# A graph and expert network on one core: rows sent as 112 and 13, and expert results scattered by token instead of stored by place and fetched by place

## The chip, the cores and the metric

The kernel runs on one core of one Trainium2 chip. The metric is the device time of one launch in microseconds (us). Before the change it is 2292.94 us, the median of three runs (2292.32 to 2293.6).

## The reference

Four blocks act on 1250 tokens of 512 features, each added to the running `x` after a layer norm. The change touches what carries rows in and out, and the second block, whose routing is this:

```python
x = x + gnn0(layernorm(x), edge_index, ...)        # graph sum, two layers with batch norm
x = x + ffn0(layernorm(x)[None], gate_w, experts)  # the block below
x = x + gnn1(layernorm(x), edge_weight, weight, src, dst)
x = x + ffn1(layernorm(x)[None], ...)              # tree of 8 leaves, 512 -> 2048 -> 512 each

# ffn0: N = 1250 tokens, 8 experts, m = N // 8 = 156 places each
cg = sinkhorn(gates)                                # 8 rounds
vals, idx = top_k(cg.T, m)                          # each expert picks 156 tokens
gate_values = vals > 0.5
outputs = einsum(routed_tokens[idx], experts) * gate_values
s = zeros(N, 512).at[idx].add(outputs)
c = zeros(N).at[idx].add(1.0)
out = s / (c + 1)
```

A plan value above 0.5 can hold for one expert only, so a token has at most one expert whose result counts. Every other row of the sum has the weight 0.

## The kernel before

A token tile is 125 rows (`TR`), and there are ten of them (`NT`). The kernel is a chain of phases, each an `nc.Block()`: in it every engine has its own program, written out by hand, and all engines meet at a barrier at its end. The order of the work is the order in which each engine's program is written. DMAs that are issued by SyncE (`sp`) run through one queue, q1, in the order of the code; those of ScalarE through q10; GpSimd's indirect ones (`q.indirect_dma_start`), whose rows are chosen by indices in SBUF, through q0.

**`phase_edges`** (L180). SyncE issues loads of constants and edges, then five loads of `x`, two tiles each (L243, `x_rows`). VectorE meanwhile builds the one-hot rows of the edges up to L308. **`phase_adjacency`** (L348) first needs all of `x`: VectorE waits for `x_loaded` and then reads its loop bounds into registers (L376), TensorE reads its bounds first and then waits for `x_loaded` (L425). TensorE then does eight small matmuls (L426), four transposes (L430), and multiplies the one-hot rows that VectorE makes (L394, L399) at L446 and L453.

**`phase_route`** (L950) makes the normalised rows `c_rows` and stores them, ten stores of one tile (L1287), into the DRAM tensor `c_d`. Its VectorE chain makes the plan, the 1280 places (8 experts of 160) and, at the end, `token_of`: which token sits at each place (L1154 to L1156), and `place_from`: at which place each token's result will lie (L1136). Empty places hold the token number 0.

**`phase_experts`** (L1374). GpSimd gathers the rows of the 1280 places from `c_d` with ten indirect DMAs of 128 rows (L1411). TensorE turns a group (`turn_x`, L1525), and works through 16 chunks of 80 places, two for each expert. Chunk `c` is evicted by ScalarE into slot `c % 4` of `y_rows` (L1458), which from chunk 4 on waits for the slot's last DMA. SyncE stores each chunk plainly to `results_d` by place (L1434). When all 16 have landed, GpSimd fetches with ten indirect DMAs of 125 rows the result of each token by its place (L1418), VectorE adds it, times the token's `share`, to `x_rows` (L1506), and the norm and the second graph sum follow (`Gather1`): its first TensorE work waits for the first tile's `A_lo` (L1333). The share is 0 for a token without an expert.

**`phase_tree`** (L1625) is the long rest. Its last step adds into `x_rows` tile by tile (L2287), and `store_out` (L1744) stores each tile as it is done, eight from SyncE's queue and two from ScalarE's.

## Time and profile before

| what | value |
|---|---|
| median of three runs | 2292.94 us (2292.32 to 2293.6) |
| the profiled execution | 2290.14 us |
| its span, first to last instruction | 2288.2 us |
| TensorE busy | 2168.5 us, 95% |
| VectorE busy | 1587.5 us, 69% |
| GpSimd busy | 623.0 us, 27% |
| TensorE's granted clock, mean | 0.979 of full |

A span is read from the first to the last instruction of one profiled execution; what lies outside it (here 1.9 us) belongs to the launch. TensorE is busy nearly all the time from 600 us on, where the tree begins. The stages that the change touches are short: the first 31 us, the stretch from 440 to 525 us, and the last 5 us.

### The profile page before, as it was taken

The numbers are of one execution on the slowest core, as the hardware profiler recorded it, in microseconds if no ns is written. First come the engines' busy times: TensorE is split into PE (matmuls) and PEld (weight loads), VectorE is DVE, ScalarE is ACT, GpSimd is POOL, SyncE is SP. The second block draws the span as 40 slices with busy tenths as digits, with TensorE's granted clock in tenths as the row PEclk, the third lists the DMA queues.
The fourth block names the chain that finished last, engine by engine and source line by source line (L and its number), as shares of the span: only waits on it lengthen the run. The fifth ranks groups of instructions, "written<-read, shape, count | busy, mean of one in ns | idle before, by whom it ended". The sixth has DMA issues, their size and how long they took to land.

```text
span 2288.2 us, 32770 instructions
## 1 busy us (share of the span) xinstructions
PE 2168.5 (95%) x11859; PEld 1901.6 (83%) x11859; DVE 1587.5 (69%) x2606; ACT 1068.2 (47%) x1857; POOL 623.0 (27%) x1066
## 2 busy tenths in 40 slices
PE   5897998588999999999999999999999999999999
PEld 4887996458858888888888888888888888888887
DVE  7994356636477667777776677777766777777665
ACT  4335335345364444455544444555444445554443
POOL 1553000111112322233223222332233223323320
PEclk9999998598999999999999999999999999999999
DMA  2000202251001111111111111111111111111111
GB/s 72 3 2 1 74 1 80 72 162 37 28 24 55 38 42 37 56 38 42 39 54 42 37 38 56 42 38 41 57 38 37 38 61 37 37 45 54 38 37 55
DMA packets 70720, 101.99 MB, mean 45 GB/s; under 512 B 5539, under 2 KB 40947, under 8 KB 70563
## 3 DMA queue, kind: packets, MB, share of 16 engines
q1 hardware_dynamic: 67263, 94.20, 12.7%
q0 software_dynamic: 3040, 5.19, 0.8%
q8 instruction: 97, 1.59, 0.3%
q10 hardware_dynamic: 260, 0.51, 0.1%
q14 instruction: 60, 0.49, 0.1%
HBM read 92.14 MB, written 7.74 MB: 44 GB/s over the span
## 4 chain that ended last, share of the span: by engine, by line
PE 73%; DVE 0%; ACT 0%; DMA 0%; issue 0%
PE psum L548 24%; PE psum L549 24%; PE psum L550 24%; PE psum L2140 1%; PE psum L2033 0%; PE psum L2023 0%; DMA w_raw<-in_w 0%; DVE w_lo L2195 0%; ACT w_forms_hi L1875 0%; PE psum L2040 0%; ACT w_hi L1884 0%; DVE x_rows L2287 0%; ACT f_rows L542 0%; DVE x_rows L2319 0%; DVE stats L506 0%
## 5 line engine op out<-in xcount | busy, mean ns | idle before, releaser
L548 PE MATMUL psum<-w_hi,hidden_hi 128*125 128x512 f32 x1280 | 503.4, 393 | 2.6 <-issue 2.4
L550 PE MATMUL psum<-w_hi,hidden_lo 128*125 128x512 f32 x1280 | 504.5, 394 | 0.0
L549 PE MATMUL psum<-w_lo,hidden_hi 128*125 128x512 f32 x1280 | 504.3, 394 | 0.0
L549 PE MATMUL psum<-x_forms_lo,w_forms_hi 128*128 128x418 f32 x1260 | 445.4, 354 | 0.0
L1816 POOL TENSOR_TENSOR w_forms<-w_raw 128x128 f32<-128x128 f32 x189 | 104.9, 584 | 1127.5 <-PE psum L550 580.2
L2287 DVE SCALAR_TENSOR_TENSOR x_rows<-psum,leaf_by_token,x_rows 125x512 f32<-125x512 f32 x320 | 233.9, 748 | 254.2 <-PE psum L550 254.2
L1913 ACT ACTIVATE hidden<-psum 128x418 f32<-128x418 f32 x315 | 162.0, 514 | 487.1 <-PE psum L550 484.9
L548 PEld LDWEIGHTS psum<-w_hi,hidden_hi 128*125 128x125 f32 x1280 | 237.4, 185 | 59.5 <-issue 3.0
L550 PEld LDWEIGHTS psum<-w_hi,hidden_lo 128*125 128x125 f32 x1280 | 236.7, 185 | 59.0
L549 PEld LDWEIGHTS psum<-w_lo,hidden_hi 128*125 128x125 f32 x1280 | 237.1, 185 | 54.1
L2260 DVE TENSOR_TENSOR hidden_lo<-hidden,hidden_hi 128x418 fp32r<-128x418 f32 (+1 forms) x384 | 255.0, 690 | 21.4 <-ACT hidden_hi L1935 21.4
L1925 ACT ACTIVATE hidden<-hidden,b1cols 128x414 f32<-128x414 f32 x315 | 201.4, 639 | 101.9 <-DVE hidden L2215 92.0
L549 PEld LDWEIGHTS psum<-x_forms_lo,w_forms_hi 128*128 128x128 f32 x1260 | 237.9, 189 | 7.7
L548 PE MATMUL psum<-x_forms_hi_late,w_forms_hi 128*128 128x418 f32 x630 | 224.1, 356 | 0.0
L548 PE MATMUL psum<-x_forms_hi_first,w_forms_hi 128*128 128x418 f32 x630 | 223.3, 355 | 0.7 <-DVE hidden L2204 0.7
L550 PE MATMUL psum<-x_forms_hi_first,w_forms_lo 128*128 128x418 f32 x630 | 222.1, 353 | 0.0
L1816 POOL TENSOR_TENSOR w_forms<-w_raw,w_forms 128x128 f32<-128x128 f32 x378 | 220.4, 590 | 4.9
L550 PE MATMUL psum<-x_forms_hi_late,w_forms_lo 128*128 128x418 f32 x630 | 221.6, 352 | 0.0
L1935 ACT ACTIVATE hidden_hi<-hidden 128x418 fp32r<-128x418 f32 (+1 forms) x384 | 204.2, 550 | 6.0
L2190 DVE TENSOR_TENSOR w_forms_lo<-w_forms,w_forms_hi 128x1792 fp32r<-128x1792 f32 x63 | 127.6, 2026 | 37.0 <-ACT w_forms_hi L1875 37.0
L1816 POOL TENSOR_TENSOR w_forms<-w_forms,w_raw 128x128 f32<-128x128 f32 x252 | 136.1, 540 | 4.9
L548 PEld LDWEIGHTS psum<-x_forms_hi_first,w_forms_hi 128*128 128x128 f32 x630 | 118.7, 188 | 8.7 <-DVE hidden L2204 1.0
(354 smaller groups left out, 3528.7 us busy)
## 6 DMA issues: line engine op xcount, KB each, us to landing
w_raw<-in_w SPq DMA_DIRECT2D x127, 512.0 KB, 3.8
expert_raw<-in_experts SPq DMA_DIRECT2D x8, 1024.0 KB, 5.5
expert_results_d<-expert_results SPq DMA_DIRECT2D x16, 160.0 KB, 4.4
x_rows<-in_x SPq DMA_DIRECT2D x5, 500.0 KB
c_rows_d<-c_rows SPq DMA_DIRECT2D x10, 250.0 KB
W_raw<-in_gnn_W SPq DMA_DIRECT2D x4, 512.0 KB, 4.1
W_raw<-in_gnn_W SPq DMA_DIRECT2D x1, 2048.0 KB, 9.7
b_by_token<-in_b SPq DMA_DIRECT2D x8, 256.0 KB, 3.8
```

The source lines that it names most:

```text
L548: t.matmul(out, stat[0], mov[0], start=start, stop=False, skip_group_check=again)
L549: t.matmul(out, stat[0], mov[1], start=False, stop=False, skip_group_check=again)
L550: return t.matmul(out, stat[1], mov[0], start=False, stop=stop, skip_group_check=again)
L1816: q.tensor_tensor(u[:, to, :], a, b, op).then_inc(w_sum, 1)
L1913: a.activation(slot_of(hid, G, b, j), g.psum[:, bank, 0:width(b)], ACT.Copy, scale=scale).then_inc(copied, 1)
L1925: a.activation(to, to, ACT.Gelu, bias=bias(G, j)).then_inc(active, 1)
L1935: a.activation(slot_of(hhi, G, b, j), slot_of(hid, G, b, j), ACT.Copy).then_inc(hi_cut, 1)
L2140: ins = t.matmul(g.psum[:, PLAIN_BANK[b][j], 0:hi - lo], g.wplain[:, k, j * 128:(j + 1) * 128], g.xf[:, k, lo:hi], start=k == 0, stop=k == ...
L2190: v.tensor_tensor(to[:, U1:U15 + 1, :], g.wsum[n % 2][:, U1:U15 + 1, :], of[:, U1:U15 + 1, :].bitcast(F32), ALU.subtract).then_inc(w_lo, 1)
L2260: v.tensor_tensor(slot_of(hlo, G, b, j), slot_of(hid, G, b, j), slot_of(hhi, G, b, j).bitcast(F32), ALU.subtract).then_inc(lo_cut, 1)
L2287: v.scalar_tensor_tensor(out=g.x_rows[:, i, :], in0=g.psum[0:TR, i % Y_BANKS, :], scalar=g.leaf[:, i, e:e + 1], in1=g.x_rows[:, i, :], op0 ...
```

## The change

Three things are changed.

1. Rows of a tile are sent as rows 0 to 111 and rows 112 to 124, in separate DMAs. The load of `x` is five DMAs of 112 rows by two tiles, and one of 13 rows by all ten. Each output tile is stored by two DMAs. The token rows that come back in the experts' phase are loaded in the same way.
2. `c_d` grows from 1250 rows to 2560. Rows 1250 to 2559 are filled from `c_rows` by two more stores in `phase_route` (values that nobody uses, but that are there), and GpSimd's first gather waits for them too.
3. A second table, `owner_of`, says for each place where its result goes: the token's own row of `c_d`, or, for an empty place, row 1280 + place. It takes four VectorE instructions at the end of `phase_route`; `place_from` goes. SyncE stores the table to DRAM and loads it back by chunk (80 by 16). After its gathers have landed, GpSimd scatters each evicted chunk into `c_d`, in place of SyncE's plain store, and SyncE then loads the ten tiles plainly from rows 0 to 1249. A token without an expert gets its normalised row back, and its share of 0 drops it.

```diff
+EVEN_ROWS = 112
+NOBODY = NG * 128
...
+            x_tiles = g.x.rearrange("(t p) d -> p t d", p=TR)
             for i in range(0, NT, 2):
-                sp.dma_start(g.x_rows[:, i:i + 2, :],
-                             g.x[i * TR:(i + 2) * TR, :].rearrange("(t p) d -> p t d", p=TR)).then_inc(g.x_loaded, 16)
+                sp.dma_start(g.x_rows[0:EVEN_ROWS, i:i + 2, :], x_tiles[0:EVEN_ROWS, i:i + 2, :]).then_inc(g.x_loaded, 16)
+            sp.dma_start(g.x_rows[EVEN_ROWS:TR, :, :], x_tiles[EVEN_ROWS:TR, :, :]).then_inc(g.x_loaded, 16)
...
-            s.mark(v.tensor_scalar(g.place_from[:, :], place[:, :], -1.0, 0.0, ALU.add, ALU.max))
...
-            s.mark(v.tensor_copy(g.token_of[:, :], token[:, :]))
+            s.mark(v.tensor_scalar(g.token_of[:, :], token[:, :], float(NOBODY), float(N - 1), ALU.add, ALU.min))
+            s.mark(v.tensor_scalar(spare[:, :], tables[:, C_G - C_Q:C_TOKEN - C_Q], 128.0, g.rowno[:, :], ALU.mult, ALU.add))
+            s.then(v.tensor_scalar(vacant[:, :], token[:, :], 0.0, None, ALU.is_equal))
+            s.then(v.tensor_tensor(spare[:, :], spare[:, :], vacant[:, :], ALU.mult))
+            s.mark(v.scalar_tensor_tensor(out=g.owner_of[:, :], in0=token[:, :], scalar=float(NOBODY), in1=spare[:, :],
+                                          op0=ALU.add, op1=ALU.add))
...
+            sp.dma_start(g.c_d[N:2 * N, :].rearrange("(t p) d -> p t d", p=TR), g.c_rows[:, :, :]).then_inc(g.c_stored, 16)
+            sp.dma_start(g.c_d[2 * N:NOBODY + NP, :], g.c_rows[0:NOBODY + NP - 2 * N, 0, :]).then_inc(g.c_stored, 16)
...
-            for i in range(4):
-                q.wait_ge(stored[i], 16 * 4)
-            q.wait_ge(x_lo, NG)
-            for t in range(NT):
-                q.indirect_dma_start(g.fetched_rows[:, t, :], None, g.results_d[:, :],
-                                     bass.IndirectOffsetOnAxis(ap=g.place_from[:, t:t + 1], axis=0),
-                                     bounds_check=NP - 1, oob_is_err=False).then_inc(fetched[t // 2], 16)
+            for i in range(NG // 2 + 1):
+                q.wait_ge(back[i], 16 if i < 2 else 32)
+            q.wait_ge(owners_in, 16)
+            for c in range(2 * NE):
+                q.wait_ge(copied, c + 1)
+                q.indirect_dma_start(g.c_d[:, :], bass.IndirectOffsetOnAxis(ap=g.owner_by_chunk[:, c:c + 1], axis=0),
+                                     g.y_rows[:, c % 4, :], None,
+                                     bounds_check=NOBODY + NP - 1, oob_is_err=False).then_inc(stored[c % 4], 16)
...
+            sp.dma_start(g.owner_d.rearrange("(g p) a -> p (g a)", p=128), g.owner_of[:, :],
+                         allow_slow_non_contiguous=True).then_inc(owners_out, 16)
+            sp.wait_ge(owners_out, 16)
+            sp.dma_start(g.owner_by_chunk[:, :], g.owner_d.rearrange("(c p) a -> p (c a)", p=CH),
+                         allow_slow_non_contiguous=True).then_inc(owners_in, 16)
...
-                sp.wait_ge(copied, c + 1)
-                sp.dma_start(g.results_d[c * CH:(c + 1) * CH, :], g.y_rows[:, c % 4, :]).then_inc(stored[c % 4], 16)
+            for i in range(4):
+                sp.wait_ge(stored[i], 16 * 4)
+            token_rows = g.c_d[0:N, :].rearrange("(t p) d -> p t d", p=TR)
+            for t in range(0, NT, 2):
+                for lo, hi in ((0, EVEN_ROWS), (EVEN_ROWS, TR)):
+                    sp.dma_start(g.fetched_rows[lo:hi, t:t + 2, :],
+                                 token_rows[lo:hi, t:t + 2, :]).then_inc(fetched[t // 2], 16)
...
     def store_out(eng, i):
         eng.wait_ge(y_added, y_count(LASTQ, i))
-        eng.dma_start(g.out[i * TR:(i + 1) * TR, :], g.x_rows[:, i, :]).then_inc(out_stored, 16)
+        for lo, hi in ((0, EVEN_ROWS), (EVEN_ROWS, TR)):
+            eng.dma_start(g.out[i * TR + lo:i * TR + hi, :], g.x_rows[lo:hi, i, :]).then_inc(out_stored, 16)
```

The order of SyncE's queue from `phase_route` to the end of the experts, before (line numbers are those of the kernel before) and then changed (its own line numbers):

```order
L1284 DMA place_tables<-in_consts_d 128x158
L1287 DMA c_rows_d<-c_rows 125x512 [waits c_normed] x10
L1290 DMA expert_raw<-in_experts 128x4x512 [waits r_w_lo] x2
L1434 DMA expert_results_d<-expert_results 80x512 [waits x_copied] x2
L1428 DMA expert_raw<-in_experts 128x4x512 [waits x_wlo]
L1432 DMA W_rows<-in_gnn_weight 128x4x512 [waits x_lo]
L1434 DMA expert_results_d<-expert_results 80x512 [waits x_copied] x6
```

```order
L1293 DMA place_tables<-in_consts_d 128x158
L1296 DMA c_rows_d<-c_rows 125x512 [waits c_normed] x10
L1297 DMA c_rows_d<-c_rows 125x10x512
L1298 DMA c_rows_d<-c_rows 60x512
L1301 DMA expert_raw<-in_experts 128x4x512 [waits r_w_lo] x2
L1438 DMA owner_of_place_d<-owner_of_place 128x10x1
L1441 DMA owner_by_chunk<-owner_of_place_d 80x16x1 [waits x_owners_out]
L1447 DMA expert_raw<-in_experts 128x4x512 [waits x_wlo] x4
L1451 DMA W_rows<-in_gnn_weight 128x4x512 [waits x_lo]
L1457 DMA fetched_rows<-c_rows_d 112x2x512 [waits x_stored2,x_stored3,x_stored1,x_stored0]
L1457 DMA fetched_rows<-c_rows_d 13x2x512
```

The chunk stores have left this queue (in the first piece the pair of chunks and one expert load stand once for four such turns), and two stores, the round trip of the owners and the plain loads have come in.

GpSimd's indirect DMAs in the experts' phase, before and then changed:

```order
L1407 UNCONDITIONAL_BRANCH [waits barrier_Pool_Activation_PE_DVE_SP_gather]
L1411 DMA rows_by_place<-c_rows_d,token_of_place 128x512 [waits c_stored]
L1411 DMA rows_by_place<-c_rows_d,token_of_place 128x512 x9
L1418 DMA fetched_rows<-expert_results_d,place_from 125x512 [waits x_stored3,x_stored2,x_lo,x_stored1,x_stored0]
L1418 DMA fetched_rows<-expert_results_d,place_from 125x512 x9
```

```order
L1420 UNCONDITIONAL_BRANCH [waits barrier_Pool_Activation_PE_DVE_SP_gather]
L1424 DMA rows_by_place<-c_rows_d,token_of_place 128x512 [waits c_stored]
L1424 DMA rows_by_place<-c_rows_d,token_of_place 128x512 x9
L1432 DMA c_rows_d<-expert_results,owner_by_chunk 2560x512 [waits x_back4,x_back5,x_back3,x_owners_in,x_back2,x_copied,x_back1,x_back0]
L1432 DMA c_rows_d<-expert_results,owner_by_chunk 2560x512 [waits x_copied] x15
```

The ten fetches have gone, and 16 scatters stand there, each behind the eviction of its own chunk; the first also waits for all gathers and for the owners.

The end of VectorE's program in `phase_route`, before and then changed:

```order
L1136 TENSOR_SCALAR place_from<-place 125x10
L1137 TENSOR_SCALAR place_i<-place 125x10
...
L1151 SCALAR_TENSOR_TENSOR share<-place,is_out 125x10
L1154 TENSOR_REDUCE token_of_place_f_8815<-psum 128x10
L1156 CAST token_of_place<-token_of_place_f_8815 128x10
```

```order
L1158 TENSOR_REDUCE token_of_place_f_8817<-psum 128x10
L1160 TENSOR_SCALAR token_of_place<-token_of_place_f_8817 128x10
L1161 TENSOR_SCALAR spare_row<-place_tables,small_consts 128x10
L1162 TENSOR_SCALAR vacant<-token_of_place_f_8817 128x10
L1163 TENSOR_TENSOR spare_row<-spare_row,vacant 128x10
L1164 SCALAR_TENSOR_TENSOR owner_of_place<-token_of_place_f_8817,spare_row 128x10
```

Behind the reduction L1154 stood one instruction, and now five do; the first row of the first piece is the one that goes.

## Rows read from the trace of the kernel before

**Rows 1.** The page: the span, and the chain that ended last by engine.

```profile
span 2288.2 us, 32770 instructions
PE 73%; DVE 0%; ACT 0%; DMA 0%; issue 0%
```

**Rows 2.** Waits (who, for whom: us, times, longest), 0 to 60, then 440 to 640.

```profile
PE psum L426 <- DMA x_rows<-in_x: 16.3, 1, 16.3
...
PE psum L548 <- DVE A_lo L1333: 17.5, 3, 16.9
```

**Rows 3.** Timeline 28 to 36 us: start, us, engine, line, operation.

```profile
28.39 0.27 DVE L308 COPY b1cols<-psum 128x128 f32<-128x128 f32 x1
30.86 1.85 PE L426 MATMUL psum<-gate,small_consts 128*125 128x8 f32 x8 [16.25 <-DMA x_rows<-in_x]
32.07 1.94 DVE L394 TENSOR_SCALAR src_onehot<-i,key 125x1280 bf16<-125x1280 f16 x4 [3.41 <-issue]
33.43 3.30 PE L446 MATMUL psum<-dst_onehot,src_onehot 125*128 x29
35.91 1.11 DVE L394 TENSOR_SCALAR src_onehot<-i,key 125x1280 bf16<-125x1280 f16 x2 [1.44 <-PE psum L446]
```

**Rows 4.** Line 376, the loads of loop bounds: ns min/median/max, first and last start.

```profile
L376 PEldq TENSOR_LOAD <-bounds x10: 587/592/781, 29.6 to 167.5; - x10
L376 DVEq TENSOR_LOAD <-bounds x10: 593/598/847, 30.8 to 165.8; - x10
```

**Rows 5.** Windows: busy PE, PEld, DVE, ACT, POOL; then PEclk, DMA share, GB/s.

```profile
8.00:10.00 2.00, 2.00 (x13) 1.71 (x12) 1.63 (x8) 0.46 (x1) 0.00 (x0) 1.00 0.46 56
28.00:30.00 2.00, 0.00 (x0) 0.00 (x0) 0.66 (x4) 0.00 (x0) 0.00 (x0) 1.00 0.33 128
506.60:507.40 0.80, 0.43 (x4) 0.19 (x2) 0.80 (x2) 0.80 (x3) 0.00 (x0) 1.00 0.70 202
```

**Rows 6.** DMA view of 8 to 10 us: packets by size.

```profile
DMA packets 690, 0.11 MB, mean 56 GB/s; under 512 B 558, under 2 KB 672, under 8 KB 690
```

**Rows 7.** The ten stores of `c_rows`: ns, first and last start.

```profile
L1287 SPq DMA_DIRECT2D c_rows_d<-c_rows x10: 250/251/505, 380.2 to 392.4; - x10
```

**Rows 8.** Timeline 441 to 461 us.

```profile
441.99 0.17 DVE L1136 TENSOR_SCALAR place_from<-place 125x10 int32<-125x10 f32 x1
442.07 0.17 DVE L1137 TENSOR_SCALAR place_i<-place 125x10 int32<-125x10 f32 x1
442.27 0.17 DVE L1138 TENSOR_SCALAR place_digits_i<-place_i 125x10 int32<-125x10 int32 x1
...
445.59 0.17 DVE L1156 CAST token_of_place<-token_of_place_f 128x10 int32<-128x10 f32 x1
446.89 1.20 POOL L1411 DMA_INDIRECT rows_by_place<-c_rows_d,token_of_place  x1 [68.88 <-issue]
450.57 1.12 PE L1525 MATMUL psum<-small_consts,rows_by_place 128*128 128x128 f32 x4 [5.23 <-DMA rows_by_place<-c_rows_d,token_of_place]
460.03 0.69 PE L1525 MATMUL psum<-small_consts,rows_by_place 128*128 128x128 f32 x4
```

**Rows 9.** Timeline from 473 us, one row of each queue or engine.

```profile
473.14 0.60 ACT L1458 ACTIVATE expert_results<-psum 80x512 f32<-80x512 f32 x1 [0.35 <-PE psum L550]
505.94 0.30 SPq L1434 DMA_DIRECT2D expert_results_d<-expert_results  x1
508.94 1.26 POOL L1418 DMA_INDIRECT fetched_rows<-expert_results_d,place_from  x1 [49.10 <-issue]
516.04 0.75 DVE L1506 SCALAR_TENSOR_TENSOR x_rows<-fetched_rows,share,x_rows 125x512 f32<-125x512 f32 x1 [7.13 <-DMA fetched_rows<-expert_results_d,place_from]
...
2283.89 0.26 SPq L1746 DMA_DIRECT2D out_rows<-x_rows  x1
```

**Rows 10.** The page's DMA issues: count, KB each, median us from issue to landing.

```profile
w_plain<-in_w SPq DMA_DIRECT2D x1, 512.0 KB, 3.4
rows_by_place<-c_rows_d,token_of_place POOLq DMA_INDIRECT x10, 3.8
```

**Rows 11.** Line 1434, the 16 chunk stores.

```profile
DMA to landing us min/median/max: 1.9/4.4/6.2
```

**Rows 12.** DMA view, 40 slices of 2280 to 2288.2 us.

```profile
GB/s 120 120 80 130 110 100 120 100 40 110 80 110 90 110 80 50 120 80 130 100 140 70 110 110 100 90 120 80 70 80 100 100 130 130 110 50 10 0 0 0
```

21 lines of the change are left out of this document (13 added, 8 removed).

## The prediction

> **What bounds the kernel now.** I read the chain of waits first, then the waits of the stretches that the change touches, then their timelines and windows. By the chain [rows 1] the kernel is TensorE's: 73% of the span are its matmuls, and nothing else has a whole per cent. The change leaves every matmul as it is. So it can only move the moments at which TensorE may start, and the moment at which the last store has landed. There are three such places. At the start TensorE waits 16.3 us for `x`; between the experts and the second graph sum it waits 16.9 us for the chain fetch, add, norm, `A_lo` [rows 2]; and the kernel ends with a store. A fourth, the gap between routing and the first gathered rows, is 5.2 us long [rows 8] and can only grow.
>
> **The start: 0.2 us gained.** The five loads of `x` run at 128 GB/s with a DMA share of 0.33 [rows 5], which is about 5 engines of 16. The 80-row store of 506.6 to 507.4 us has a share of 0.70 and 202 GB/s in a window that it doesn't fill. 125 is 5 times 25, 80 is 16 times 5: I infer from these rows that rows are shared out evenly over the largest number of engines up to 16 that divides them. Then 112 rows go over 16, 13 over 13, and the load takes about half its time: 2.56 MB in 10 to 12 us in place of 20, so that `x` is in SBUF by about 22 us in place of 30.8.
> The Trainium skill, "DMA: Bandwidth & Descriptors", section "Why a DMA increments its semaphore by 16 and not by 1", gives the same division rule. By it the 13 rows use 13 engines; the sum goes by the rows, which show only 125 and 80, and the case in which 13 behaves otherwise is a rival below.
> What is late then? VectorE ends the edges' phase at 28.66 us (28.39 + 0.27) [rows 3]. TensorE's load of loop bounds, which doesn't wait for `x`, starts at 29.6 us [rows 4]: it already shows how early the next phase can begin. With 0.6 us for the load and 0.4 for what follows (VectorE's load starts at 30.8, and its first instruction at 32.07, so 1.27 us in all, of which 0.6 is the load), TensorE is ready at about 30.65. It starts at 30.86 now. So 0.2 us is gained of 16.3. VectorE gains more: its load can start at 29.6 too, 1.2 us earlier. But VectorE has at once to wait for TensorE's first 20 matmuls (1.44 us, until 35.91) [rows 3], so that TensorE's start decides. I take 0.2; the ends are 0 and 1.2, VectorE's gain.
>
> **The end of routing: 0.5 us lost.** Chained small VectorE instructions follow each other by 0.20 us (442.07 to 442.27), unchained ones by 0.08 (441.99 to 442.07) [rows 8]. Behind `token_of` come four new ones, up to the end of `owner_of`: two at 0.08, two at 0.22 (the reduction at 445.37 and the copy at 445.59 stand 0.22 apart): 0.6 us. `place_from` gives back 0.08. All engines meet at the barrier behind it, so 0.5 us is on the path; ends 0.4 and 0.8.
>
> **The larger `c_d`: nothing.** 1310 more rows, 2.68 MB, over 5 engines at 128 GB/s: 20 to 21 us behind the ten stores, whose last is issued at 392.4 [rows 7] and has landed by about 404. They end near 425 and the gather starts at 446.89 [rows 8]: 20 us of slack is the cover. The load of the third expert, which stands behind them in the queue, isn't used before the experts' phase. Without that cover each us would be paid in full.
>
> **The round trip of the owners: 0.3 us lost.** 1280 packets of 4 bytes out and 1280 back, 80 for each of 16 engines. No such store stands in the trace. The nearest row is 8 to 10 us: 690 packets, 558 of them under 512 B, with a DMA share of 0.46, so 0.46 x 2 us x 16 / 690 = 21 ns for each [rows 5, 6]. The other end is a whole 2 KB packet: 2048 B at a fifth of 128 GB/s, 80 ns. Each DMA then takes 80 x 21 to 80 x 80 ns, 1.7 to 6.4 us, and about 1.5 us around it (the 80-row store, 5 packets for each engine, lands in 1.9 at best [rows 11]). The owners are in at 447 + 6.4 = 453 to 447 + 16 = 463 us. Nobody waits until the first scatter must have landed for chunk 4 to be evicted, at 473.14 [rows 9]. What is paid is the quarrel with the first gathers: TensorE waits for group 0 until 450.57 [rows 8], and its 8 packets for each engine share the engines with the store's. Some 8 small packets between them are 0.2 to 0.6 us: I take 0.3, ends 0 and 2. Later groups have slack, since group 2 is turned at 460.03 only [rows 8].
>
> **Scatter and plain load: 1.8 us gained.** Now: last store issued at 505.94, landed 1.9 us later, GpSimd's first fetch at 508.94, 1.1 us after the landing (behind the barrier too it needs 1.1: 446.89 against the end of VectorE's last instruction at 445.76 [rows 8]), VectorE at 516.04 [rows 9, 11]. Changed: GpSimd sees the last eviction at 505.9, just before the store's issue, and starts its scatter at 506.8 (I take 0.9, since one wait stands there in place of five). It lands as a gather does, after 3.8 us [rows 10]: 510.6. SyncE issues 112 x 2 and 13 x 2 rows, 512 KB together. `w_plain`, of the same size, lands in 3.4 us [rows 10]; 0.3 us for the second issue: 514.3. So 1.8 us earlier than 516.04. Ends: a scatter of 2.7 us (0.8 us of issue, and 1.9) and a load of 3.0 give 512.5, 3.5 us gained; a scatter as slow as the slowest chunk store, 6.2 us [rows 11], and a load of 4.5 give 517.5, 1.5 us lost. GpSimd's earlier scatters keep pace (about 2 us each against a chunk every 3.2 us). The later pairs come faster than VectorE takes them, and all behind it up to the tree moves as one piece.
>
> **The last store: 1.5 us gained.** 250 KB over 5 engines at about 100 GB/s are 2.5 us; the data ends at 2280 + 37 x 0.205 = 2287.6 [rows 12], and the span at 2288.2. Over 16 engines the 224 KB take 0.9 us at 250 GB/s, and the 13 rows one packet more behind an issue of 0.3 us. 2.5 - 0.9 gives 1.6, less what the second issue shows: 1.5. Ends 0.3 and 1.8.
>
> **The sum.** -0.2 + 0.5 + 0.3 - 1.8 - 1.5 = -2.7 us. The profiled execution takes 2290.14 us, so 2287.4 as profiled. The median of the runs stands 2.8 us above it, and the forecast goes with the median: 2292.94 - 2.7 = 2290.2. A measurement of this kernel tells 0.2%, 4.6 us, from no change; 2.7 us lies inside.
>
> **Rivals.**
> *Faster: the DMAs in the middle are short ones.* The fetch by index goes, and with 5 packets for each engine the scatter is nearer to the store's 1.9 us than to the gather's 3.8. For it speaks that a gather carries 128 rows and 0.2 us more of issue; against it, that the chunk stores' median is 4.4 us [rows 11]. Then 3.5 from the middle, 1.8 at the end and VectorE's 1.2 at the start, less 0.5: -6.0, 2286.9 us.
> *The 13 rows stay on one engine.* Then a pair's second DMA puts 26 packets behind 14: 40 x 80 ns = 3.2 us in place of 1.2, and the middle loses 0.2 in place of gaining 1.8. At the end 20 packets at 100 ns are 2.0 us, and 0.3 is left. The start has room (70 + 130 packets x 80 ns = 16 us from 10.3 is 26.3, before 29.6). Sum: -0.2 + 0.8 + 0.2 - 0.3 = +0.5, 2293.4 us. Against it: 125 rows don't stay on one engine either.
> *Slower: the owners come late and the ring of four fills.* The scatter of chunk 0 must be issued by 473.14 - 3.8 - 0.9 = 468.4. From 446.6, less 2 x 1.5 us, that leaves 18.8 us for 160 packets: at over 117 ns for each, ScalarE waits, and TensorE behind it. At 200 ns the owners come 13 us late, and the time is 2290.2 + 13 = 2303 us. The rows give 21 to 80 ns, but for no 4-byte store.
> The Trainium skill, "DMA: Bandwidth & Descriptors", section "Specifications", says that below 512 B a DMA engine does a read and a modified write. No row here shows what that costs; if it doubled the 80 ns of a whole packet to 160, the sum would be 7 us worse by it. This rule speaks against the change, and it is that rival's reason.
>
> **How the numbers follow.** My forecast has 0.61, the faster rival 0.22, one engine for 13 rows 0.09, late owners 0.08. The forecast's own range is 2287.6 to 2292.5. To leave no more than 2 in 10 out, the range goes down to the faster rival and up past the one-engine case: 2286.6 to 2294.0. Faster by over 0.2% (below 2288.4) is the faster rival and a strip of the forecast, 0.25; slower by over 0.2% (above 2297.5) is late owners, 0.08; the rest, 0.67, is within.
>
> **What would show it right or wrong.** Start: `x` landed by 22 us, first matmul at L426 (new line 429) near 30.65. Routing: the first gather 0.5 us after its old distance from the reduction. Owners: `owner_by_chunk` landed by 463. Middle: from the last eviction to VectorE's first add 8.4 us in place of 10.1. End: from the last add to the end 2.9 us in place of 4.4. The forecast is wrong if VectorE decides the start, if a scatter takes over 5 us, or if ScalarE waits for a scatter.

## The result, and the profile after

The changed kernel takes 2295.64 us (median of 20 runs, 2294.69 to 2298.22), the kernel before 2291.80 on the same chip (20 runs, 2290.58 to 2293.6): a ratio of 1.0019, interval 1.0013 to 1.0025. It is slower by 3.8 us. That is outside the range of the prediction, whose upper end was 2294.0, and the time moved the other way: forecast were 2.7 us less, from the median of three runs of the kernel before (2292.94), which lies 1.1 us above the median of twenty. The profiled executions are 2290.14 us before and 2295.32 us after, the spans 2288.2 and 2293.5. So the two profiles lie 5.2 us apart, the medians 3.8: the profiled execution of the kernel before is one of its faster ones, 1.7 us below its median, that of the kernel after is 0.3 below its own.

The page of the kernel after, span and chain, answers to [rows 1]: the chain is TensorE's as before.

```profile
span 2293.5 us, 32798 instructions
PE 73%; issue 0%; ACT 0%; DVE 0%
```

The timeline at the start answers to [rows 3], line 429 to the old 426:

```profile
28.11 0.27 DVE L311 COPY b1cols<-psum 128x128 f32<-128x128 f32 x1
30.01 1.94 DVE L397 TENSOR_SCALAR src_onehot<-i,key 125x1280 bf16<-125x1280 f16 x4 [1.63 <-issue]
30.37 1.84 PE L429 MATMUL psum<-gate,small_consts 128*125 128x8 f32 x8 [16.05 <-issue]
32.93 4.12 PE L449 MATMUL psum<-dst_onehot,src_onehot 125*128 x40
35.41 1.11 DVE L397 TENSOR_SCALAR src_onehot<-i,key 125x1280 bf16<-125x1280 f16 x2 [3.00 <-PE psum L449]
```

TensorE starts 0.5 us earlier, and what ends its wait is no longer the DMA of `x`. VectorE starts 2.06 us earlier and gives all but 0.5 of it back in the wait for TensorE (3.00 in place of 1.44).

The timeline from the end of routing to the first scatter answers to [rows 8] (1438 and 1441 are the store and the load of the owners, 1424 the gather, 1549 the first transposes, 1482 the eviction of a chunk, 1432 the scatter):

```profile
445.06 0.17 DVE L1160 TENSOR_SCALAR token_of_place<-token_of_place_f 128x10 int32<-128x10 f32 x1
446.12 0.37 SPq L1438 DMA_DIRECT2D owner_of_place_d<-owner_of_place  x1
446.97 1.21 POOL L1424 DMA_INDIRECT rows_by_place<-c_rows_d,token_of_place  x1 [69.31 <-issue]
456.55 0.34 SPq L1441 DMA_DIRECT2D owner_by_chunk<-owner_of_place_d  x1
459.44 2.05 PE L1549 MATMUL psum<-small_consts,rows_by_place 128*128 128x128 f32 x8 [14.62 <-DMA rows_by_place<-c_rows_d,token_of_place]
467.63 0.59 ACT L1482 ACTIVATE expert_results<-psum 80x512 f32<-80x512 f32 x1 [5.51 <-PE psum L553]
470.78 0.93 POOL L1432 DMA_INDIRECT c_rows_d<-expert_results,owner_by_chunk  x1 [10.85 <-DMA owner_by_chunk<-owner_of_place_d]
480.45 0.60 ACT L1482 ACTIVATE expert_results<-psum 80x512 f32<-80x512 f32 x1 [0.35 <-PE psum L553]
```

Here is the loss. The gather is issued at 446.97, where it was before (446.89), but TensorE gets its first rows at 459.44 in place of 450.57: 8.9 us late. The fifth eviction stands at 480.45 against 473.14 [rows 9], 7.3 us later, and from there on everything is. (The 1.6 us between the two figures are the granted clock: at its half level until 7.2 us behind the first transposes here, 459.44 to 466.6, and until 9.6 us behind them before, 450.57 to 460.2.) What ends the wait of the fifth eviction is TensorE ("<-PE psum"), and by the view of the scatters (line 1432) no eviction waited for one. From issue to landing, the views of lines 1424, 1438 and 1441 give, in this order (minimum, median, maximum):

```profile
DMA to landing us min/median/max: 10.4/11.2/12.4
DMA to landing us min/median/max: 10.4/10.4/10.4
DMA to landing us min/median/max: 13.2/13.2/13.2
```

A gather took 3.8 us in the median before [rows 10]. The DMA view of the same 12 us, 446 to 458, says what the engines were busy with (queue: packets, MB, share of the time of 16 engines; `q0` carries the gathers, `q1` the DMAs of SyncE). Before:

```profile
DMA packets 554, 1.83 MB, mean 152 GB/s; under 512 B 108, under 2 KB 108, under 8 KB 554
q0 software_dynamic: 554, 1.83, 51.0%
```

After:

```profile
q0 software_dynamic: 86, 0.32, 69.7%
q1 hardware_dynamic: 1296, 0.01, 4.9%
```

A packet of the gathers' queue takes 0.51 x 192 / 554 = 0.18 us in the mean before (12 us of 16 engines are 192 us) and 0.697 x 192 / 86 = 1.56 us after. The packets of the 4-byte store themselves are charged with 0.049 x 192 / 1296 = 0.007 us. The small store is cheap by its own packets; what it costs stands in the packets of the others.

The mean hides how. The gathers' large packets carry 4096 B each, and the trace has the time of every one. Of those that start in these 12 us, the 446 before take 0.16 us in the median and 0.85 at most; the 78 after take 0.83 in the median, and six of them 6.6 to 8.3 us. The store's own packets all start between 447.02 and 447.84, and yet it lands only at 456.5. So a few packets stand still for as long as the store takes to land.

The middle, timeline, answers to [rows 9]:

```profile
512.62 0.59 ACT L1482 ACTIVATE expert_results<-psum 80x512 f32<-80x512 f32 x1 [2.18 <-PE psum L553]
514.01 0.91 POOL L1432 DMA_INDIRECT c_rows_d<-expert_results,owner_by_chunk  x1 [1.86 <-ACT expert_results L1482]
516.70 4.52 SPq L1457 DMA_DIRECT2D fetched_rows<-c_rows_d  x10
520.84 0.75 DVE L1530 SCALAR_TENSOR_TENSOR x_rows<-fetched_rows,share,x_rows 125x512 f32<-125x512 f32 x1 [4.62 <-DMA fetched_rows<-c_rows_d]
528.43 0.69 PE L551 MATMUL psum<-A_hi,d_rows_hi 125*128 125x418 f32 x1 [14.10 <-DVE A_lo L1344]
```

From the start of the last eviction to VectorE's first add it is 520.84 - 512.62 = 8.22 us; before it was 516.04 - 505.31 = 10.73. The wait of TensorE for `A_lo` falls from 16.9 us [rows 2] to 14.1. The scatter and the plain load do what was forecast, and more: 2.5 us.

The end, the last add of the tree (VectorE, line 2312):

```profile
2290.07 0.75 DVE L2312 SCALAR_TENSOR_TENSOR x_rows<-psum,leaf_by_token,x_rows 125x512 f32<-125x512 f32 x1 [2.04 <-PE psum L553]
```

From its start to the end of the span it is 3.43 us; before, from 2283.11 to 2288.2, it was 5.09. So 1.66 us gained.

One piece is left. From TensorE's first matmul of the middle to the last add, where nothing was changed, it takes 2283.11 - 523.92 = 1759.19 us before and 2290.07 - 528.43 = 1761.64 after: 2.45 us more. The timeline of TensorE shows it just behind a pause in the last steps of the second graph sum, where the tree begins. Before:

```profile
636.02 0.62 PE L2023 MATMUL psum<-small_consts,f_rows 125*128 125x125 f32 x4 [2.23 <-issue]
636.47 2.98 PE L2140 MATMUL psum<-f_xT,w_plain 128*128 128x418 f32 x8
```

After:

```profile
640.32 0.72 PE L2048 MATMUL psum<-small_consts,f_rows 125*128 125x125 f32 x4 [2.23 <-issue]
640.83 4.61 PE L2165 MATMUL psum<-f_xT,w_plain 128*128 128x418 f32 x8
```

The same eight matmuls after the same pause take 4.61 us in place of 2.98. The windows of the kernel after (columns as in [rows 5]: busy PE, PEld, DVE, ACT, POOL, then the granted clock of TensorE) show the clock at its half level, 1.2 of 2.4 GHz, in two stretches behind pauses:

```profile
638.10:640.30 2.20, 0.00 (x0) 0.02 (x1) 1.62 (x8) 1.14 (x3) 0.00 (x0) 1.00 0.00 0
640.70:644.10 3.40, 3.40 (x8) 1.82 (x6) 3.31 (x8) 2.05 (x4) 0.00 (x0) 0.50 0.00 0
...
685.07:688.48 3.41, 3.22 (x8) 2.56 (x9) 2.60 (x6) 0.00 (x0) 0.00 (x0) 0.50 0.49 153
```

The second stands behind a pause of 2.35 us. The kernel before has both pauses (2.23 and 2.36 us) and no such stretch behind either. Its window:

```profile
637.70:641.10 3.40, 3.40 (x13) 1.92 (x13) 2.20 (x5) 1.35 (x3) 0.00 (x0) 1.00 0.00 0
```

Both kernels have one more stretch at half clock between the middle and the last add, 3.41 us long, from 600.16 before and from 603.15 after; it cancels in the comparison.

In the profiled executions the sum is: +7.3 up to the last eviction, -2.5 to the first add, -0.3 to the first matmul, +2.45 to the last add, -1.7 to the end: +5.3 us.

### The profile page after: what moved, and what is told of

The parts are those of the page before. It is cut to its first block, busy times and chain, and to the rows that moved or that the text cites. A ratio compares the mean times of both kernels' runs of the same rounds, so it can differ in the third digit from the quotient of the medians.

```text
span 2293.5 us, 32798 instructions
## 1 busy us (share of the span) xinstructions
PE 2170.1 (95%) x11859; PEld 1902.5 (83%) x11859; DVE 1587.7 (69%) x2609; ACT 1068.3 (47%) x1857; POOL 627.9 (27%) x1072
## 4 chain that ended last, share of the span: by engine, by line
PE 73%; issue 0%; ACT 0%; DVE 0%
PE psum L551 24%; PE psum L552 24%; PE psum L553 24%; PE psum L2165 1%; PE psum L2058 0%; PE psum L2048 0%; ACT w_forms_hi L1900 0%; PE psum L2065 0%; DVE x_rows L2312 0%; ACT f_rows L545 0%; DVE x_rows L2344 0%; DVE stats L509 0%; DVE hidden L2229 0%; ACT w_forms_hi L1898 0%; ACT w_forms_hi L1896 0%
```

## Experiments

Times are medians, with the number of runs; each ratio is to the kernel before in the runs of the same chip (2291.57, 2291.81 and 2291.60 us in the three groups e1 to e4, e5 to e8 and e9 to e12). The theory at the start: the round trip of the owner numbers in packets of 4 bytes holds up the gathers, and all the rest of the change gains.

### e1: the kernel before with the rows split, and nothing else

```diff
...
+                sp.dma_start(g.x_rows[0:EVEN_ROWS, i:i + 2, :], x_tiles[0:EVEN_ROWS, i:i + 2, :]).then_inc(g.x_loaded, 16)
+            sp.dma_start(g.x_rows[EVEN_ROWS:TR, :, :], x_tiles[EVEN_ROWS:TR, :, :]).then_inc(g.x_loaded, 16)
...
+        for lo, hi in ((0, EVEN_ROWS), (EVEN_ROWS, TR)):
+            eng.dma_start(g.out[i * TR + lo:i * TR + hi, :], g.x_rows[lo:hi, i, :]).then_inc(out_stored, 16)
```

> The kernel before with the 112 and 13 rows at the load of x and at the output stores only. Theory (the split gains at both ends, as the trace after shows it: first edge matmuls 0.5 us earlier, 3.4 in place of 5.1 us from the last add to the end): 2.2 us less than before, ratio 0.9990, gathers land in 3.8 us. Rival (the two ends gain nothing by themselves, and the changed kernel's shorter end comes from something else): no difference, tail 5.1 us. Second rival (the doubled number of output DMAs disturbs the tree's weight loads): slower than before.

2288.61 us (11 runs, 2287.04 to 2290.40), ratio 0.9987 (0.9978 to 0.9996): 3.0 us faster. The profile has the first matmuls of the edges at 33.00 (33.43 before [rows 3]) and 3.4 us from the last add to the end (5.09): 2.1 of the 3.0 us. The split is a gain by itself.

### e2, e5: the kernel before with the store of the owners' size, and half of it

Nobody reads what it stores and nobody waits for it before the last chunk.

```diff
         def _(sp):
+            sp.dma_start(g.owner_d.rearrange("(g p) a -> p (g a)", p=128)[:, 0:10], g.token_of[:, 0:10],
+                         allow_slow_non_contiguous=True).then_inc(owners_out, 16)
```

> The kernel before with nothing but the store of 1280 four-byte numbers added at the start of the experts' phase (token_of goes out; nobody reads it and nobody waits for it until the phase's end). Theory (these packets hold the DMA engines against the gathers): the store lands after about 10 us, the first gather lands at 8 to 11 us in place of 3.6, TensorE's first transpose waits 12 to 15 us in place of 5.2, and the time is 7 us above before. Rival (the larger c_d, whose rows are gathered, or its 2.7 MB of extra stores, make the gathers slow): gathers land in 3.8 us and the time is that of before, within 1 us.

2297.94 us (6 runs, 2296.28 to 2298.54), ratio 1.0029 (1.0017 to 1.0041): 6.4 us slower. The store lands after 11.2 us, the gathers after 5.4, 8.1 and 10.6. TensorE, in the timeline of e2:

```profile
447.44 0.37 SPq L1425 DMA_DIRECT2D owner_of_place_d<-token_of_place  x1
458.85 1.11 PE L1529 MATMUL psum<-small_consts,rows_by_place 128*128 128x128 f32 x4 [12.10 <-DMA rows_by_place<-c_rows_d,token_of_place]
```

One instruction that nobody waits for brings the whole loss. Is it the number of packets? In e5 the slices are `[:, 0:5]`: 640 packets in place of 1280.

> The kernel before with half of the store added: five of the ten columns, 640 four-byte packets. Theory (the cost goes by the number of small packets): the store lands after about 6 us in place of 11.2, the first gathers are late by half as much, time 3 to 4 us above before. Rival (any strided store of this kind blocks the engines for a fixed time): 6 to 7 us above before, as with 1280.

2298.39 us (6 runs, 2297.55 to 2301.14), ratio 1.0034 (1.0021 to 1.0046). Half the packets, the same loss: the store lands after 11.5 us, the gathers after up to 11.5. The timeline of e5:

```profile
446.39 0.37 SPq L1425 DMA_DIRECT2D owner_of_place_d<-token_of_place  x1
458.82 1.97 PE L1529 MATMUL psum<-small_consts,rows_by_place 128*128 128x128 f32 x8 [13.12 <-DMA rows_by_place<-c_rows_d,token_of_place]
```

Between 640 and 1280 packets the cost doesn't go with their number, and so the way in which the prediction priced the store (a time for each packet, times 80) is wrong. In both runs, too, most of the gathers' 4096 B packets of 446 to 458 us are as fast as before (0.16 to 0.18 us in the median), and single ones take up to 7.5 us (e2) and 7.2 us (e5).

### e6: the kernel before with a load of 1280 numbers of 4 bytes

```diff
...
+            sp.dma_start(g.dummy[:, :], g.b1.rearrange("e h -> (e h)")[0:NP].rearrange("(g p) -> p g", p=128),
+                         allow_slow_non_contiguous=True).then_inc(owners_out, 16)
```

> The kernel before with a load of 1280 four-byte numbers from DRAM at the start of the experts' phase, which nobody uses, in place of the store. Theory (a small packet costs its time whichever way it goes): lands after 6 to 10 us, gathers late, time 3 to 7 us above before. Rival (only small writes to DRAM are slow, since less than a full burst is read and written back): the load lands in 3 to 4 us, gathers in 3.8 to 4.5 us, time within 1 us of before.

2291.55 us (10 runs, 2290.22 to 2293.75), ratio 1.0001 (0.9991 to 1.0010). The DMA view, 446 to 458 us, of e6:

```profile
q0 software_dynamic: 526, 1.75, 51.6%
q1 hardware_dynamic: 1296, 0.01, 5.0%
```

1296 packets again, with nearly the same share as in the kernel after, at the same moment; but the gathers' packets stay at 0.516 x 192 / 526 = 0.19 us. The load lands in 2.2 us and the first transposes start at 450.96. So it isn't small packets as such: it is small packets that are written to DRAM. The Trainium skill, "DMA: Bandwidth & Descriptors", section "Specifications", says that below 512 B a DMA engine reads and writes back. The costly store of e2 fits that; the row makes no difference between a store and a load, though, and the load of e6 pays nothing. The page gives no price, and that the price falls on the other queue's packets isn't in that section. The same page, section "Back-pressure in remote DMA", says of writes between cores that stalled writes also stall the other queues of their engine. No run here has writes between cores, but e2 and e5 look like that. That this, or the reading back, is the mechanism isn't shown. Nor is it known whether the 4 bytes do it, or that neighbouring pieces of one stretch of DRAM come from different engines: no run has small pieces that lie far apart.

### e3: the kernel after without the round trip

VectorE computes the scatter's table from two constants, and nothing goes to DRAM and back for it. The table names the spare rows 1280 + place: this kernel leaves out the way of the experts' results to their tokens, and its output isn't the reference's. Number and size of the scatters are those of the kernel after.

```diff
-            sp.dma_start(g.owner_d.rearrange("(g p) a -> p (g a)", p=128), g.owner_of[:, :],
...
-            sp.dma_start(g.owner_by_chunk[:, :], g.owner_d.rearrange("(c p) a -> p (c a)", p=CH),
...
+                v.tensor_scalar(g.owner_by_chunk[:, :].rearrange("p (e h) -> p e h", h=2)[:, :, h], g.place0[0:CH, :],
+                                float(NOBODY + h * CH), g.rowno[0:CH, :], ALU.add, ALU.add).then_inc(owners_in, 1)
```

> The changed kernel without the round trip of the owners: VectorE writes a table of the spare rows 1280 + place in two instructions, so that the experts' results are scattered to spare rows (left out: their way to the tokens' own rows), with the same DMAs of the same sizes. Theory: gathers land in 3.8 us as before, chunks start 7 to 8 us earlier than in the changed kernel, no eviction waits; the time is 7 to 8 us below the changed kernel, 2288, 4 us below before. Rival (larger c_d): gathers still land at 10 to 12 us and the time stays within 1 us of the changed kernel, 2295.6.

2289.34 us (10 runs, 2287.28 to 2290.76), ratio 0.9988 (0.9979 to 0.9997). Against the kernel after (1.0019) it is 6 to 7 us faster: what e2 costs alone. The gathers land in 3.5, 3.9 and 4.2 us (minimum, median, maximum), with the larger `c_d` in place.

### e4: the owners by rows

TensorE transposes the table before the store and after the load, so that it goes out as 10 packets of 512 B and comes back as 16 of 320 B. A copy on ScalarE and one on VectorE belong to it, and the scatters wait for the table turned back. Everything else is the kernel after.

```diff
-            sp.dma_start(g.owner_d.rearrange("(g p) a -> p (g a)", p=128), g.owner_of[:, :],
-                         allow_slow_non_contiguous=True).then_inc(owners_out, 16)
+            sp.dma_start(g.owner_d.rearrange("(g p) -> g p", p=128), g.vecrows[0:NG, :]).then_inc(owners_out, 16)
...
+            t.transpose(g.psum[0:NG, 7, 0:128], g.owner_of[:, :], g.ident[:, :]).then_inc(owner_step, 1)
...
+                        t.transpose(g.psum[0:CH, 7, 0:2 * NE], g.b1rows[0:2 * NE, 0:CH],
+                                    g.ident[0:2 * NE, 0:2 * NE]).then_inc(owner_step, 1)
```

> The changed kernel with the owners turned on TensorE first, so that they go out as 10 packets of 512 B and come back as 16 of 320 B, and are turned again (two transposes, a copy on ScalarE, one on VectorE). Theory (it is the number of small packets that costs): gathers land in 3.8 to 4.2 us, the owners are there by 453 us, time 7 us below the changed kernel: 2288 to 2289, ratio to before 0.9983. Rival (any second DMA beside the gathers, or the wait of the scatters for the owners, costs it): gathers late by several us and the time above 2293. Rival (larger c_d): as the changed kernel, 2295.6.

2288.96 us (12 runs, 11 of them 2287.14 to 2290.71 and one, unexplained, 5535.89; without it the median is 2288.90), ratio 0.9989 (0.9981 to 0.9998). The timeline of e4:

```profile
446.27 0.30 SPq L1440 DMA_DIRECT2D owner_of_place_d<-vecrows  x1
446.37 1.20 POOL L1425 DMA_INDIRECT rows_by_place<-c_rows_d,token_of_place  x1 [69.54 <-issue]
447.55 0.33 SPq L1442 DMA_DIRECT2D b1rows<-owner_of_place_d  x1
449.94 1.11 PE L1554 MATMUL psum<-small_consts,rows_by_place 128*128 128x128 f32 x4 [3.99 <-DMA rows_by_place<-c_rows_d,token_of_place]
512.64 0.75 DVE L1535 SCALAR_TENSOR_TENSOR x_rows<-fetched_rows,share,x_rows 125x512 f32<-125x512 f32 x1 [4.43 <-DMA fetched_rows<-c_rows_d]
520.35 0.69 PE L551 MATMUL psum<-A_hi,d_rows_hi 125*128 125x418 f32 x1 [14.02 <-DVE A_lo L1344]
```

The same 5 KB to the same DRAM, and the gathers land in 3.5, 4.1 and 4.8 us (3.6, 3.8 and 4.4 in the kernel before). The loss is in the form of the store, and it goes.

But e4 should beat e1, since its middle is shorter by what scatter and plain load gain, and it doesn't: 2288.96 against 2288.61. Where that went is the question of e9 to e12.

### e7: the kernel after, the store held back until two gathers have landed

```diff
+            sp.wait_ge(back[0], 16)
+            sp.wait_ge(back[1], 16)
             sp.dma_start(g.owner_d.rearrange("(g p) a -> p (g a)", p=128), g.owner_of[:, :],
```

> The changed kernel with the store of the owners issued only when the first two gathers have landed. Theory: the first two groups are turned at once (chunk 0 starts 7 us earlier than in the changed kernel), but groups 2 and 3 are late by some us, and the owners come at about 452 + 10 + 13 = 475 us: the first scatter lands at 480, ScalarE's eviction of chunk 4 waits 5 to 7 us, and so does TensorE. Time 1 to 5 us below the changed kernel, above before or even with it. Rival (the wait for the owners never matters, since the later chunks catch up): 2288 to 2289 us, as with the round trip by rows.

2295.95 us (10 runs, 2292.76 to 2297.35), ratio 1.0019 (1.0009 to 1.0029): nothing gained. TensorE starts at 449.82, but the store, at 451.47, lands after 11.4 us, the load behind it after 10.2, and the ten gathers after 3.5, 13.3 and 14.6 us (minimum, median, maximum). The first scatter stands at 474.10 in place of 470.78, and now the ring of four is full. The timeline of e7:

```profile
474.10 2.92 POOL L1432 DMA_INDIRECT c_rows_d<-expert_results,owner_by_chunk  x1 [14.93 <-DMA owner_by_chunk<-owner_of_place_d]
482.42 0.59 ACT L1484 ACTIVATE expert_results<-psum 80x512 f32<-80x512 f32 x1 [8.53 <-DMA c_rows_d<-expert_results,owner_by_chunk]
```

This is the prediction's slow rival, made by hand. With the store early the price is paid by the gathers, with the store late by the ring; moving it doesn't avoid it.

### e8: e4 with the tokens' rows loaded as whole tiles of 125

```diff
-                for lo, hi in ((0, EVEN_ROWS), (EVEN_ROWS, TR)):
-                    sp.dma_start(g.fetched_rows[lo:hi, t:t + 2, :],
-                                 token_rows[lo:hi, t:t + 2, :]).then_inc(fetched[t // 2], 16)
+                sp.dma_start(g.fetched_rows[:, t:t + 2, :],
+                             token_rows[:, t:t + 2, :]).then_inc(fetched[t // 2], 32)
```

> The version with the owners sent by rows, but with the five plain loads of token rows as whole tiles of 125 rows by two, not as 112 and 13. Theory (125 rows go over 5 engines only): the first pair takes 4 us to move in place of 1.3, VectorE's first add comes 10.5 to 11 us after the last eviction in place of 8.0, and later pairs arrive every 4 us, faster than VectorE takes two tiles (5.6 us); time 2.5 to 3 us above the version by rows. Rival (the fixed part of a DMA decides, and the split gains nothing in the middle): VectorE's add at 8.0 to 8.5 us, time unchanged.

2292.69 us (10 runs, 2291.63 to 2294.51), ratio 1.0006 (0.9996 to 1.0015): 0.9 us above the kernel before of its group, where e4 is 2.6 below, so 3.5 us slower than e4. Last eviction to first add 10.33 us (507.96 to 518.29) against 8.02 in e4. VectorE then waits 1.07 us more for the second pair of tiles, at 522.30, which it doesn't in e4. Without the split, scatter and plain load save only 0.4 us of the 10.73 up to the first add and lose it again up to TensorE's first matmul (527.06 - 507.96 = 19.10 us; before 523.92 - 505.31 = 18.61). The middle's gain needs the split.

### e9, e12: the pause filled

The pause of 2.23 us stands ahead of the eighth turn, where TensorE waits for ScalarE's `f_rows`. Three matmuls whose result is overwritten fill it, in e4 (e9) and in e1 (e12).

```diff
+            for _ in range(3):
+                t.matmul(g.psum[:, 4, 0:384], g.ident, g.small[:, 0:384], start=True, stop=True)
             t.wait_ge(plain_in, 16)
             turn(7)
```

> The owners' rows version (e4, 2288.96 us by its runs, a span of 2285.3 in its profile) with three matmuls of 128x384 on TensorE in the pause of 2.23 us ahead of the first tree matmuls, where it waits for the eighth f_rows of ScalarE. They write a bank of PSUM that the next work overwrites. Theory: the granted clock of 0.50 just behind this pause (633.20 to 636.61, 1.6 us) comes of the pause, and it is what eats most of what the shorter middle gave. Then the matmuls behind it run at full clock, last add and end come 1.3 to 1.7 us earlier: 2287.4 (2287.0 to 2287.9). Rival: the fall is a chance of the profiled execution and its time is not in the timed ones: no change, 2288.9 (2288.5 to 2289.3), with or without the fall in the profile. Second rival: the three matmuls last longer than the pause or wait for their weights, and the eighth turn comes late: 2289.3 to 2290.

> The kernel before with only the rows sent as 112 and 13 at start and end (e1, 2288.61 us), and the three matmuls of e9 in the same pause. Its profile has no fall of the clock there. By the theory there is nothing to win: 2288.6 (2288.2 to 2289.0). If the matmuls themselves help or hurt in another way (the work behind them starts warm, or late), it shows here by the same amount as in e9.

e9: 2285.86 us (10 runs, 2284.78 to 2287.35), ratio 0.9976 (0.9967 to 0.9986), 3.1 us faster than e4 (2.6 against 5.7 us below the kernel before of its group). e12: 2288.39 us (10 runs, 2286.39 to 2289.87), ratio 0.9985 (0.9975 to 0.9994): no change against e1. The timeline of e9:

```profile
631.01 2.10 PE L2183 MATMUL psum<-small_consts 128*128 128x384 f32 x6
633.40 0.62 PE L2061 MATMUL psum<-small_consts,f_rows 125*128 125x125 f32 x4 [0.29 <-issue]
633.86 2.98 PE L2178 MATMUL psum<-f_xT,w_plain 128*128 128x418 f32 x8
```

The eight matmuls are back at 2.98 us, and the second fall is gone too although its pause (2.36 us, up to 676.66) wasn't filled. So e9 gains about twice what was expected of it, which was the first fall alone. From the first matmul of the middle to the last add e9 takes 2279.73 - 521.48 = 1758.25 us, e4 2281.89 - 520.35 = 1761.54, and e1, which has the same stretch and no fall at these pauses, 2283.37 - 525.29 = 1758.08. So the theory of the clock holds, the rival (a chance of the profiled execution alone) falls: the timed runs gain what the profile shows. And between e9 and e12, both without falls at these pauses, the gain of scatter and plain load shows in the timed runs: 2288.39 - 2285.86 = 2.5 us, the routing's 0.6 paid. The traces have 2.5 up to the first add and 0.3 up to the first matmul, less 0.6: 2.2.

### e10: both pauses filled, the owners' arithmetic behind the routing

```diff
-            s.mark(v.scalar_tensor_tensor(out=g.owner_of[:, :], in0=token[:, :], scalar=float(NOBODY), in1=spare[:, :],
...
+            s.then(v.scalar_tensor_tensor(out=g.owner_of[:, :], in0=g.token_f[:, :], scalar=0.0, in1=g.owner_of[:, :],
+                                          op0=ALU.is_equal, op1=ALU.mult))
+            v.scalar_tensor_tensor(out=g.owner_of[:, :], in0=g.token_f[:, :], scalar=float(NOBODY), in1=g.owner_of[:, :],
```

> As e9, with three such matmuls in the second pause too (2.36 us, ahead of the first matmul of the second layer), and with the arithmetic of the owner numbers moved behind the last instruction of the routing on VectorE, where the gathers have begun. The routing's end should come back to what it is in the kernel before: 0.3 to 0.5 us earlier. Theory of the clock: both falls gone, 1.4 to 1.6 us each in the profile, so 2285.6 (2285.0 to 2286.4). Rival that the falls are only of the profiles: 2288.5 (2288.0 to 2289.0), 0.4 below e4 by the arithmetic alone.

2284.78 us (9 runs, 2283.62 to 2287.77), ratio 0.9975 (0.9965 to 0.9985). From the table of places to the first gather it is 1.29 us (448.06 to 449.35), as before (445.59 to 446.89); the kernel after needs 1.91 (445.06 to 446.97). So this step of the prediction is confirmed by its undoing. The runs lie in two groups, five at 2283.6 to 2284.8 and four at 2287.0 to 2287.8. The profiled one is of the upper group: its routing is late by 2 to 3 us against e9's (448.06 against 445.15), and its windows show a lower clock far ahead of all in which it differs from e9. Of e10:

```profile
185.00:200.00 15.00, 9.12 (x32) 8.53 (x32) 7.26 (x18) 11.55 (x19) 7.14 (x6) 0.66 0.00 1
205.00:220.00 15.00, 12.74 (x68) 11.30 (x67) 7.80 (x15) 5.77 (x12) 2.61 (x2) 0.89 0.00 1
```

Of e9:

```profile
185.00:200.00 15.00, 9.48 (x39) 8.59 (x40) 8.18 (x19) 12.95 (x21) 7.91 (x7) 0.77 0.01 1
205.00:220.00 15.00, 12.79 (x78) 11.67 (x77) 8.08 (x16) 5.59 (x11) 1.54 (x2) 1.00 0.01 1
```

No fall stands behind the two filled pauses, but the one near 600 us lasts 6.8 us (596.49 to 603.32) in place of 3.4 in e9. By the medians e10 is 6.8 us below the kernel before on the same chip and 10.9 below the kernel after; by its ratio, which takes both groups in, the first of these is 5.7. e10 and e9 (ratio 0.9976) can't be told apart.

### e11: e4 with its first add made 1.4 us late

```diff
+                    if t == 0:
+                        for _ in range(2):
+                            s.then(v.tensor_tensor(g.fetched_rows[:, 0, :], g.fetched_rows[:, 0, :],
+                                                   g.fetched_rows[:, 0, :], ALU.max))
```

> The owners' rows version (e4) with two maxima of a tile of 125x512 with itself on VectorE ahead of the first add of the middle: the first add starts 1.4 to 1.5 us later than it could, 514.1 instead of 512.64. If nothing behind depends on when the stage starts: 2290.4 (2290.0 to 2290.8), the delay at its full price. If the two falls of the clock depend on how the pauses lie in time, moving everything by 1.4 us takes one or both away and gives the delay back: 2288.9 (2287.3 to 2289.4), and the profile shows no fall near 638 us.

2289.06 us (10 runs, 2287.27 to 2290.71), ratio 0.9989 (0.9980 to 0.9998): as fast as e4, where the full price would be 2290.4. But the profile has both falls (from 635.55 and from 679.93), against what the explanation by the falls asked for, and it shows the delay at full price at the add (the maxima from 515.22, the add at 516.67). A third fall is the one that is missing: e4 has one from 595.65, e11 none there (590 to 605 us are at 1.00), and from the middle's first matmul to the eight matmuls it takes 635.49 - 524.25 = 111.24 us against 632.90 - 520.35 = 112.55. That would be enough to give the delay back, but it is one profile. 1.4 us is hardly more than two such medians can tell apart. Inconclusive: that a delay is given back isn't shown, and neither is what it is in time that makes a pause bring a fall.

## Why the prediction was wrong, point by point

**What bounds the kernel: right.** TensorE in both, and the time moved only at the places named. One that was not named moved too: the clock behind two pauses that were there before.

**The start, 0.2 forecast, 0.5 found.** The reason was right: `x` is in by about 21 us (in the windows of the kernel after, the DMA share is 0.73 at 18 to 20 us and 0.03 at 20 to 22) and no longer decides. The size was low by 0.3. Its working doesn't hold either: of the 1.27 us from VectorE's load to its first instruction 0.6 is the load, which leaves 0.67 and not 0.4 for what follows, and with 0.67 nothing would have been gained. What it had as fixed moved: TensorE's load of loop bounds starts at 29.3 in place of 29.6.

**The end of routing, 0.5 forecast, 0.6 found** (1.30 to 1.91 us from the table to the gather), and e10 takes it back.

**The larger `c_d`, nothing: right.** The second extra store occupied SyncE for 20.2 us from 394.2, and no one waited for it; in e3 and e4, which have it, the gathers land as before.

**The round trip, 0.3 forecast, 7.2 found: the step that failed.** The prediction says: "What is paid is the quarrel with the first gathers", and prices it as "some 8 small packets between them", 0.2 to 0.6 us, with ends 0 and 2. The place was right, the price was more than 20 times too small, and the upper end of 2 less than a third of it. Two assumptions stand behind it. First, that a small packet costs its engine a time of its own and the others only that time; the rows taken for it (21 ns each at 8 to 10 us) were loads. By the traces the small store's packets take 7 ns each, and the gathers' packets next to them go from 0.18 to 1.56 us in the mean, since a few of them stand for up to 8.3 us. Second, that the cost goes with the number of packets; e5, with half of them, costs the same. The bound had to come from rows of another kind, since there was no small store in the trace: the sentence "no such store stands in the trace" was there, and the range drawn from it was still one of loads and whole packets. Of the signs that the prediction named, this is the one that spoke: `owner_by_chunk` was to be in by 463 and landed at 469.7.

**The slow rival: the right suspect at the wrong place.** It had the price of a 4-byte store as its condition, but let it be paid only by the ring of four and by a store of more than 117 ns for each packet. Its condition was even met: 10.4 and 13.2 us, less 1.5 for each DMA, are 129 ns for each of 160 packets, and the first scatter is issued at 470.78, later than the 468.4 that it allowed. But the gathers had paid first, and chunk 4 was itself 7.3 us late. In e7, where they are spared, the ring does pay. As an explanation of the result it is wrong (no eviction waits for a scatter in the kernel after), as a warning it was worth more than its 0.08.

**Scatter and plain load, 1.8 forecast, 2.5 found.** GpSimd issues 0.8 us after the last eviction has ended (forecast 0.9); the scatter is seen landed after 2.7 us (514.01 to 516.70), not 3.8; the load takes 4.1, not 3.7. Over all 16 scatters the landing takes 3.9 us in the median and up to 7.0, so a quick last one is no rule. The faster rival had the direction of the scatter right. e8 shows what the forecast had left implicit: the gain needs the split.

**The last store, 1.5 forecast, 1.7 found.** Start and end together are e1: 3.0 us in the medians, 2.1 in the profile.

**Rows on engines: right.** That 13 rows don't stay on one engine is what e1's end and e8's loss show.

**What the forecast had no term for: +2.45 us of clock.** A shorter wait ahead moved nothing in the pauses behind it, and yet the clock fell behind them. In the profiles the fall at the first pause stands in each of the six with scatter and plain load where the pause is left open (after, e3, e4, e7, e8, e11) and in none of the five with the fetch and an open pause (before, e1, e2, e5, e6). With it filled (e9, e10, e12) there is none. The second pause doesn't divide so cleanly: two of the five with the fetch, e5 and e6, have a fall behind it (from 686.49 and from 679.43). And these are single executions. Of the 88 runs of the kernel before in the three groups, 22 have a mean granted clock of 0.976 or 0.977 and take 2293.1 us in the mean, 53 have 0.979 or more, as the profiled one, and take 2290.9: the kernel before, too, loses clock in some of its executions; where, no trace shows. Its profiled stretch of 1759.19 us is also 1.1 longer than that of e1 (1758.08) with the same falls, for no reason that was found. The better measure of the clock's price is e9 against e4, 3.1 us in the runs.

The account in medians: the split gives 3.0 us (e1). Scatter and plain load, the routing's 0.6 paid, give 2.5 (e9 against e12). The clock takes back 3.1 (e9 against e4). The store of 4-byte pieces costs 6.3 to 6.7 (the kernel after against e3 and e4). 2291.8 - 3.0 - 2.5 + 3.1 + 6.5 = 2295.9; measured are 2295.64. Each of these differences is uncertain by about 1 us, and they come from different chips.

## What to carry to other kernels

A store to DRAM in 4-byte pieces was not priced here by its bytes, its packets or its own rows in the trace: look at what else the DMA engines carry at that moment. Turn such a table on TensorE first and send it as rows; e4, with its two small transposes, can't be told from e3, which has no round trip at all (2288.96 and 2289.34 us). And where a kernel is TensorE's, look at the granted clock behind its pauses, even ones as short as the 2.23 us here, before you believe or refuse a gain elsewhere: three throwaway matmuls in one pause gave back 3 us where the clock fell behind it (e9), and nothing where it didn't (e12).

## What the runs showed of the hardware

- Beside the gathers, a store of 1280 or of 640 pieces of 4 bytes from 128 partitions to DRAM lands in 10.4 to 11.5 us (after, e2, e5, e7), a load of 1280 such pieces in 2.2 us (e6), and 10 rows of 512 B with the same content can be read back 1.3 us after their issue (e4: 446.27 and 447.55).
- While such a store is under way, the packets on the gathers' queue take 1.56 us in the mean in place of 0.18 (after against before), and single ones of 4096 B up to 8.3 us in place of 0.85; beside a small load the mean stays at 0.19 (e6).
- A load of 4-byte pieces that comes behind such a store, among delayed gathers, lands after 13.2 us (after) or 10.2 (e7). Its part in the loss was not separated from the store's; e2 shows that the store alone is enough.
- Behind a pause of TensorE of 2.23 us the granted clock goes to its half level in the kernel after (640.7 to 644.1 us), and the same pause in the kernel before leaves it at 1.00. In e9, where it is filled, the later one leaves the clock alone too. What decides whether it falls stays open; e11 didn't settle it.
